# Gathering a pair of chunks only after the pair two places ahead has landed, in both edge attentions of a graph network

## What is computed

```python
# layer 0, for every edge (row -> col), H = 8 heads of 32
scores = sum(Q[col] * (K[row] + rel), axis=-1) / sqrt(DK)
attn = softmax of scores over the edges that end in one node
out = segment_sum(attn * V[row], col)
# layer 1: the reference has H = 4 heads of 64 and
score = leaky(alpha_src[src] + alpha_dst[dst])
attn = softmax of score over the edges that end in one node
h = segment_sum(attn * val[src], dst)
```

## Time and profile before

| | |
|---|---|
| median of 3 runs, not profiled | 2918.83 us (2916.1 to 2921.84) |
| span of the profiled execution | 3243.1 us |
| granted TensorE clock, mean over the span | 0.936 |
| PE / DVE / ACT / POOL busy in the span | 84% / 49% / 33% / 30% |
| gathers, layer 0 and layer 1 | 416 and 416, 947 ns of POOL each |
| layer 0 attention, from first gather to last `match` | 166.0 to 831.1 us |
| layer 1 attention, from first gather to last gather | 1005.0 to 1667.0 us |

### The profile page before, as it was taken

How to read it: one execution, slowest core, us unless ns; L and a number is a source line. 1 busy time by engine, 2 the same in 40 slices (tenths; PEclk the granted TensorE clock), 3 DMA queues, 4 the chain that set the end, 5 groups by cost and what they waited for, 6 DMA issues and landing times. The chain is left out here.

```text
span 3243.1 us, 53070 instructions
## 1 busy us (share of the span) xinstructions
PE 2724.4 (84%) x17114; PEld 1944.9 (60%) x17114; DVE 1576.1 (49%) x2779; ACT 1084.9 (33%) x3016; POOL 969.2 (30%) x1020
## 2 busy tenths in 40 slices
PE   6748888888861777777776999999999998999998
PEld 4637777777741666666663555555555656565665
DVE  8357777777653767666757224141514224111123
ACT  1014444444430556555562222040404034111111
POOL 2346666666335556565634001010101000000000
PEclk7869999999985899999996999999999999999999
DMA  6568888888333476666664433424252514444433
GB/s 246 174 191 266 254 262 252 257 254 258 109 93 70 88 122 131 121 124 121 122 101 154 142 102 120 135 90 130 80 149 69 150 37 138 124 118 115 127 106 96
DMA packets 332504, 470.20 MB, mean 145 GB/s; under 512 B 155942, under 2 KB 243062, under 8 KB 331588
## 3 DMA queue, kind: packets, MB, share of 16 engines
q1 hardware_dynamic: 269364, 286.33, 33.0%
q0 software_dynamic: 59088, 176.67, 18.9%
q10 hardware_dynamic: 3776, 3.80, 0.4%
HBM read 412.95 MB, written 55.50 MB: 144 GB/s over the span
## 5 line engine op out<-in xcount | busy, mean ns | idle before, releaser
L827 POOL DMA_INDIRECT e_from_src<-vk,src x416 | 393.9, 947 | 302.5 <-PE e_part_ps L1019 161.0
L827 POOL DMA_INDIRECT e_from_src<-val,src x416 | 394.1, 947 | 276.5 <-PE e_part_ps L1019 129.1
L2321 PE MATMUL sum_ps<-room,high 128*128 128x391 f16 x1900 | 470.3, 331 | 2.4 <-DVE z_t L2498 2.4
L2321 PE MATMUL sum_ps<-room,low 128*128 128x391 f16 x1824 | 454.0, 331 | 0.0
L2719 PE MATMUL sum_ps<-room,high 128*128 128x391 f16 x1200 | 389.4, 329 | 0.5 <-DVE x L2863 0.5
L1017 PE MATMUL e_part_ps<-e_onehot,e_from_src 128*128 128x129 f32 x1664 | 304.2, 309 | 96.4 <-issue 51.7
L2719 PE MATMUL sum_ps<-room,low 128*128 128x391 f16 x1152 | 379.3, 329 | 0.0
L1017 PEld LDWEIGHTS e_part_ps<-e_onehot,e_from_src 128*128 128x128 f32 x1664 | 241.2, 208 | 125.7 <-issue 69.6
L1121 ACT ACTIVATE sums<-e_part_ps 128x384 f32 x416 | 205.2, 493 | 328.6 <-PE e_part_ps L1019 234.0
L1017 PE MATMUL e_part_ps<-x,e_from_src 128*128 128x129 f32 x1664 | 273.2, 287 | 36.0 <-issue 24.7
L897 DVE TENSOR_TENSOR e_from_src<-e_from_src,e_fixed 128x2048 f32<-128x2048 f32 x104 | 237.5, 2284 | 113.2 <-ACT e_fixed L1102 70.7
(11 more groups left out here) (421 smaller groups left out, 4418.3 us busy)
## 6 DMA issues: line engine op xcount, KB each, us to landing
room<-adj SPq DMA_DIRECT2D x128, 977.5 KB, 4.9
e_window<-q_part SPq DMA_DIRECT2D x416, 128.0 KB
room<-adj SPq DMA_DIRECT2D x32, 488.8 KB
room<-adj SPq DMA_DIRECT2D x32, 391.0 KB
adj<-e_counts SPq DMA_DIRECT2D x8, 1250.0 KB
adj<-e_counts SPq DMA_DIRECT2D x8, 1193.8 KB
e_from_src<-vk,src POOLq DMA_INDIRECT x416
e_from_src<-val,src POOLq DMA_INDIRECT x416
```

The lines of the kernel that those rows point to most:

```text
L827: nc.gpsimd.indirect_dma_start(from_src[:, b, j, :], None, by_src, bass.IndirectOffsetOnAxis(ap=keep["src"][:, g * G + j:g * G + j + 1], a ...
L2321: mm = nc.tensor.matmul(sum_ps[KH * n + m][:, 0:AN], part[:, t, m * P:(m + 1) * P], slab[s][:, n, k * AN:(k + 1) * AN], start=(t == 0 and ...
```

## The change

POOL gets one more wait, in front of the first gather of every pair from the third pair of a layer on: the pair that was issued two places ahead must have landed. To be able to wait for a pair in layer 1 too, that layer gets four semaphores per buffer like layer 0 (16 in place of 4), and `take_scores` of layer 1 waits for four semaphores in place of one. Which rows are gathered, where they go, and the order of issue stay as they are.

```diff
-        LANDED = 1 if layer else PAIRS
-        src_in = [sems(nc, ctx, *(f"e{layer}_src_in{b}_{i}" for i in range(LANDED))) for b in range(RING)]
+        src_in = [sems(nc, ctx, *(f"e{layer}_src_in{b}_{i}" for i in range(PAIRS))) for b in range(RING)]
...
                     if it:
                         pool.wait_ge(chunk_summed[b], G * (it - 1) + j + 2)
+                    if j % 2 == 0 and g * PAIRS + j // 2 >= 2:
+                        of, pair = divmod(g * PAIRS + j // 2 - 2, PAIRS)
+                        pool.wait_ge(src_in[of % RING][pair], 32 * (of // RING + 1))
                     nc.gpsimd.indirect_dma_start(
                         from_src[:, b, j, :], None, by_src,
-                        bass.IndirectOffsetOnAxis(ap=keep["src"][:, g * G + j:g * G + j + 1], axis=0)).then_inc(src_in[b][j * LANDED // G], 16)
+                        bass.IndirectOffsetOnAxis(ap=keep["src"][:, g * G + j:g * G + j + 1], axis=0)).then_inc(src_in[b][j // 2], 16)
...
                 else:
-                    v.wait_ge(src_in[b][0], 16 * G * it + 16 * G)
+                    for pair in range(PAIRS):
+                        v.wait_ge(src_in[b][pair], 32 * (it + 1))
                     v.wait_ge(spread[r], g // 2 + 1)
```

## The result

The changed kernel takes 3229.54 us, median of 4 runs (3226.2 to 3234.33). The kernel before took 2917.56 us beside it, median of 4 (2916.1 to 2921.84). The ratio is 1.1072 with a 95% interval of 1.1052 to 1.1092: slower by 312 us, where I had forecast 2914 and a range up to 2932.

A forecast was written before the change was run, and what follows sets the result against it. It took TensorE as busiest in both attentions, waiting for windows in the openings, with POOL slack. Layer 0: 0, stores -6, VectorE +0.5 made -5.5 us, scaled by 0.90 to -5: 2914 us, range 2900 to 2932.

The forecast's parts named there:

- The pair's share of time, 3.06 us: Layer 0's steady part: a pair of gathers takes 3.06 us, a group 12.23, with POOL idle 41%.
- a factor of 0.90: Whole kernel: 2918.83 / 3243.1 scaled the summed -5.5 us from profiled to timed, giving -5 us.
- L = 3.7 us (3.2 to 4.2): Layer 0: time from issue of a pair's second gather to its landing, under the 4.87 us available on average.
- The Trainium skill's estimate: Layer 0: a 262 KB gather takes about 2.0 us plus bytes over 436e3, 2.6 us, so the wait never bites.
- Cost 0, hidden by the lead of the ring: Layer 0's steady part: short holds of POOL cost 0, as readers have 10 to 14 us.
- Layer 1 between the stores: Layer 1, judged from its opening burst: L about 2.5 us is under 3.75, so the wait costs 0.
- Layer 1 at the stores: cost 0, gain 6 us: Layer 1's 16 count stores: held gathers catch up at cost 0; stores ending earlier gain 0.4 us each, -6 us.
- New instructions 0.5 us: Layer 1: VectorE's three more waits per group cost 0.5 us; POOL's wait and twelve semaphores 0.
- Slower: Rival, chance 0.2: the new wait becomes layer 0's bound from L = 4.87 us, giving 2939 or 2956 us.
- Stores freed: Rival, chance 0.2: layer 1's gathers compete with count stores; 16 to 28 us go, 2893 to 2903 us.
- SP freed: Rival, chance 0.12: slower gathers let SP issue layer 0's opening windows sooner; 10 to 20 us, 2900 to 2910.
- What would show it: Signs of error: `match` or line 864 waiting for gathers, layer 0 groups over 12.4 us, opening waits shortened over 5 us.

The follow-up runs named there:

- experiment 1: The kernel before, unedited, profiled once more (the second trace of before, span 2912.8 us): 2912.48 us, ratio 0.9991.
- after: The changed kernel's first profiled execution, span 3228.2 us; that execution took 3229.92 us.
- second trace of the change: The changed kernel run and profiled once more without an edit: 3233.08 us, ratio 1.1071 to the kernel before.
- earlier trace: The first trace of the kernel before, which the prediction read: span 3243.1 us, that execution's own time not known.
- experiment 7: The changed kernel without POOL's new wait, keeping layer 1's 16 semaphores and VectorE's waits: 2914.59 us, ratio 0.9994 to the kernel before.
- experiments 3 and 11: Changed kernel with the wait in layer 1 only: 3043.58 us, ratio 1.0438; with two pairs back in layer 1, eight in layer 0: 3069.18 us, 1.0516.

## Why the prediction was wrong

- **The pair's share of time, 3.06 us.** This step failed first, and all others rest on it. I read 12.23 us per group from one trace and took POOL's 41% idle for slack. The execution of experiment 1, which took as long as the timed ones, issues a pair each 2.50 us with no slack at all. The sign was there: the span was 324 us over the median of the runs. I spread that difference evenly, by a factor of 0.90 on a sum near zero, instead of asking where it lies. I had also seen SP crawl in the starts, and took it for a property of the kernel. A factor of 0.90 on 12.23 gives 11.0 us; the truth was 10.0, because 278 of the 330 us lay in the gathers.
- **L = 3.7 us (3.2 to 4.2).** It was read where the layer's and the burst's gathers stop and less else moves. From the pace it is 5.28. Half of the missing 1.6 us I had at nothing: 0.74 us pass from the landing until POOL's next gather starts. The other half is the landing itself, about 4.5 us in place of 3.7. By my own formula, (1.25 + 5.28) / 2 = 3.27 exceeds 3.06, so this error alone would have turned the sign. The DMA share of 0.80 spoke for a longer one; I named it only as a rival's argument. That 44 us (208 x 0.21) would already have been a clear loss.
- **The Trainium skill's estimate** (DMA: Bandwidth & Descriptors, Anatomy of one DMA) was 2.6 us for a landing, and by it the wait would never bite in layer 0. The traces have more: the shortest landing recorded in layer 0 is 3.7 us in after and 3.3 us in its second trace, and the pace speaks for about 4.5.
- **"Cost 0, hidden by the lead of the ring", layer 0.** A lead hides a late gather, not a lower rate. With both POOL and TensorE full, a pair each 3.264 us in place of 2.494 costs 208 x 0.770 = 160 us at any lead. Measured: +160.2.
- **Layer 1 between the stores**: nearly right. A landing takes 2.8 us, I had 2.5, and with the 0.74 us behind it that is just under 3.75. POOL still loses some 25 us, in short waits.
- **Layer 1 at the stores: cost 0, gain 6 us.** I had the mechanism (gathers held back while q0 is silent) and its length of about 6 us, and then let them "catch up". POOL can't, since it has no spare time: every hold is lost, some 136 us over 15 stores (5.9 to 10.8 us each, one in two parts of 4.5 and 5.0), and with the short waits layer 1 takes 160.6 us more. The gain was looked for in ACT's wait of 28.5 us. Of that, 17.6 us stood in the earlier trace rows under another releaser, a gather of layer 0, and were never shown to be a wait for a store; in the second trace ACT waits 8.5 us for stores.
- **New instructions 0.5 us**: right within what can be told (experiment 7).
- **The rivals.** "Slower" had the right place and rule, the wait as bound of layer 0, but decided from L = 4.87 us where 3.75 was the point at 2.50 us per pair, and was priced at 20 to 37 us instead of 160. It left out layer 1, which costs as much. The range, up to 2932, left out both times that I had worked out for this rival, 2939 and 2956, and not only its heavy end, as I wrote. "Stores freed" and "SP freed" both lived on waits that are mostly not there in the second trace of before: 8.5 us for stores, and for windows in the openings 14.7 us in three waits in layer 0 and 5.1 us in layer 1, where I had 27.8 and 30.1.
- **What would show it** did: line 852 and line 867 wait 164.5 and 151.1 us for gathers, and a group of layer 0 takes 679.0 / 52 = 13.1 us, over the 12.4 named.

On the order of the queues, the Trainium skill (DMA: Bandwidth & Descriptors, Queues, rings and completion order) has each engine go round between queues packet by packet. The trace of after disagrees once more, as the earlier trace rows had: in 1108 to 1112 q1 moves 1052 packets and q0 none, with gathers issued and not landed. Whether their packets already stood in the engines' queues by then, no run here shows.

Open are why the stores take 1.7 to 1.9 us longer when layer 0's waits are in the program, and what made SP slow in the first trace of before; it was not seen in any other.

## What to carry to other kernels

When the span of a profiled execution is 11% over the timed median, find where the difference lies before reading any slack from it: an engine that showed as busy 59% of a stretch had no spare time in an execution as fast as the timed ones. A limit on transfers in flight costs nothing while the landing, and the 0.74 us until the engine goes on, fit into the time in which the rest of them is issued, here (d - 1) x 2.50 + 1.25 us for d pairs. The landing must be taken in the middle of the layer's traffic and under its longest disturbance, here a 1.25 MB store. A buffer ahead of a reader hides lateness but never a rate, so compare the new rate with the engine's old one first.

## What the runs showed of the hardware

- A gather of 128 rows occupies POOL for 0.95 + 0.30 = 1.25 us whether a row has 2048 bytes or 1056.
- In layer 0 of after, at 241 GB/s beside windows, 5.28 us pass on average from a pair's second gather to the gather that waits for it (5.31 in the second trace of the change). The landings recorded, of few gathers, are 3.7 to 6.5 us and 3.3 to 5.7 us; in layer 1, away from stores, 2.7 to 3.0 us.
- A gather of POOL that was held starts a median of 0.74 us after the landing that it waited for (both traces of the change, where landings are recorded).
- A store of 1.25 MB from the `counts` buffer, in packets under 512 bytes, ran beside a queue q0 that moved no packet for 4 us, and such stores land after 14.3 us; halved stores land after 7.2 to 7.7.
- Two programs that differ in wait instructions of an earlier layer differ by 1.9 us in the median landing of the same store (12.6 and 14.5 us, experiments 3 and 11).
- SP's register load had a median of 700 ns in the starts of one profiled execution, and 267 ns in the openings of the other, at the same rate of gathers.
